# First stage of a fused gated cross-attention kernel: a ring of 15 chunks, tanh over runs of five chunks, weight rows spread over the batches

## The reference

```
txt_proj = jnp.einsum('btd,de->bte', textual_features, Ws)
feat_proj = jnp.einsum('bfd,de->bfe', features, W)
h = jnp.tanh(txt_proj[:, None, :, :] + feat_proj[:, :, None, :] + b[None, None, :, :][..., 0, :])
rho = jnp.einsum('bftd,d->bft', h, w[:, 0])
rho = rho + (1.0 - qm)[:, None, :] * NEG
att = jax.nn.softmax(rho, axis=-1)
txt_h = jnp.einsum('bft,btd->bfd', att, textual_features)
w_s = jnp.tanh(jnp.einsum('bfd,od->bfo', txt_h, Wcw) + bcw)
b_s = jnp.tanh(jnp.einsum('bfd,od->bfo', txt_h, Wcb) + bcb)
return w_s * features + b_s
```

## Time and profile before

| | us |
|---|---|
| median of 3 runs | 2029.7 |
| lowest, highest run | 2028.11, 2811.3 |
| the profiled execution | 2029.61 |
| its span in the trace | 2027.6 |
| main loop of stage A: first unit's tanh starts, last starts | 93.5, 951.3 |
| granted clock over the span | 0.965 of 2.4 GHz |

### The profile page before, as it was taken

How to read it: one execution, slowest core, us unless ns; L and a number is a source line. 1 busy time by engine, 2 the same in 40 slices (tenths; PEclk the granted TensorE clock), 3 DMA queues, 4 the chain that set the end, 5 groups by cost and what they waited for, 6 DMA issues and landing times.

```text
span 2027.6 us, 24744 instructions
## 1 busy us (share of the span) xinstructions
PE 1626.4 (80%) x9638; PEld 733.6 (36%) x9638; DVE 1744.2 (86%) x2631; ACT 1483.3 (73%) x1109; POOL 633.2 (31%) x476
## 2 busy tenths in 40 slices
PE   6868955697668857875789959999999968888886
PEld 4212211131112212221344436666666623433332
DVE  5899999999999988896778768888887779999994
ACT  4899999999999999998344735555554466665660
POOL 1000000000000000000351247666666537677773
PEclk9999999999999999999799979999999989999997
DMA  5001100020000010000676752333331111111111
GB/s 195 1 18 35 58 6 1 21 78 16 1 1 6 21 47 1 1 11 1 238 278 219 253 167 90 107 110 104 110 102 61 58 39 53 55 52 52 63 52 53
DMA packets 104294, 143.67 MB, mean 71 GB/s; under 512 B 7790, under 2 KB 61166, under 8 KB 103794
## 3 DMA queue, kind: packets, MB, share of 16 engines
q1 hardware_dynamic: 104178, 142.09, 20.9%
HBM read 91.74 MB, written 50.33 MB: 70 GB/s over the span
## 4 chain that ended last, share of the span: by engine, by line
ACT 42%; PE 33%; DVE 12%; POOL 7%; issue 4%; DMA 2%; POOLq 0%; SPq 0%; DVEq 0%; ACTq 0%
ACT unit L514 38%; PE psum L1624 6%; PE psum L1658 5%; POOL hidden L1806 5%; PE psum L1610 4%; PE psum L1009 3%; PE psum L1015 3%; DVE unit L423 2%; POOL h L1789 2%; PE psum L1634 2%; PE psum L1683 2%; DVE psum L1416 2%; DMA xblk<-xnT_scratch 2%; DVE hmax_parts L1425 2%; PE psum L1651 1%
## 5 line engine op out<-in xcount | busy, mean ns | idle before, releaser
L514 ACT ACTIVATE unit<-unit 128x4096 f32<-128x4096 f32 x244 | 857.5, 3615 | 0.5 <-DVE unit L423 0.3
L423 DVE TENSOR_SCALAR unit<-feat_proj,text_proj 128x1024 f32<-128x1024 f32 x976 | 668.0, 749 | 66.3 <-PE psum L639 64.5
L639 PE MATMUL psum<-unit,w_pad 128*32 128x512 f32 x3904 | 471.6, 601 | 236.3 <-ACT unit L514 236.3
L639 PEld LDWEIGHTS psum<-unit,w_pad 128*32 128x32 f32 x3904 | 102.3, 109 | 556.6 <-ACT unit L514 399.5
L680 POOL TENSOR_SCALAR red<-red 128x8 f32<-128x8 f32 x4 | 2.0, 508 | 531.5 <-DVE red L321 531.5
L1683 PE MATMUL psum<-xq_block,w_q 128*128 128x512 bf16 x512 | 132.7, 405 | 38.8 <-ACT hidden L1577 38.8
L1789 POOL TENSOR_TENSOR h<-h,arow 128x512 f32<-128x512 f32 x96 | 128.2, 1344 | 92.2 <-ACT h L1558 92.2
L1720 PE MATMUL psum<-w_q,hidden_q 128*128 128x512 fp8e4 x512 | 122.2, 394 | 29.7 <-DVE hidden_q L1449 29.7
L1806 POOL TENSOR_TENSOR hidden<-hidden,srow 128x2048 f32<-128x2048 f32 x32 | 130.4, 4074 | 27.1 <-ACT srow L1593 21.0
L680 POOL TENSOR_SCALAR rstd<-mv 128x8 f32<-128x8 f32 (+1 forms) x5 | 1.7, 334 | 412.4 <-DVE mv L216 412.4
L547 PE MATMUL psum<-xnT,W_sb 128*128 128x512 f32 x256 | 125.2, 617 | 2.1 <-ACT xnT L465 2.1
(11 more groups left out here) (243 smaller groups left out, 2780.0 us busy)
## 6 DMA issues: line engine op xcount, KB each, us to landing
h_scratch<-h SPq DMA_DIRECT2D x44, 512.0 KB, 3.1
hin<-h_scratch SPq DMA_DIRECT2D x32, 704.0 KB, 4.6
xin<-in_x SPq DMA_DIRECT2D x8, 1024.0 KB, 6.7
tern_in<-in_w1T SPq DMA_DIRECT2D x16, 512.0 KB, 5.5
tern_in<-in_w2T SPq DMA_DIRECT2D x16, 512.0 KB, 5.5
x<-in_x SPq DMA_DIRECT2D x16, 512.0 KB, 3.6
x_scratch<-x SPq DMA_DIRECT2D x32, 256.0 KB, 2.0
x3in<-x_scratch SPq DMA_DIRECT2D x31, 256.0 KB, 2.8
```

Of the source, the lines that this page charges most:

```text
L423: ins = ve.tensor_scalar(units[:, n % 3, k, :], FP[:, bi % 2, k, :], TP[:, k, n:n + 1], None, ALU.add)
L514: ac.activation(units[:, n % 3], units[:, n % 3], ACT.Tanh).then_inc(unit_tanh, 1)
L639: mm = te.matmul(psum[k * TG:(k + 1) * TG, 3 + 2 * grp + half, :], w_pad[:, k, TG - 1 - tt:2 * TG - 1 - tt], units[:, n % 3, k, half * BAN ...
```

## The change

Stage A's ring is cut into 15 chunks instead of three units, and the loops on ACT and PE go by **runs** of five chunks instead of units of four. What a chunk holds and what is added to it stays.

- DVE still adds four chunks per unit, but signals `unit_added` after each, and waits by chunk: chunk q needs the run that held chunk q - 15 to be through PE.
- ACT: 976 chunks in 195 runs of five, and one of one; one ACTIVATE over 5120 columns per run, when its five chunks are added.
- PE: per run, both halves, in each the five chunks in order; `unit_mm` counts runs. A run's chunks are at column groups k, k+1, k+2, k+3, k. What stood behind a unit's calls (`besides`) now stands behind the run that holds the unit's last chunk.
- ROW_SLOTS: four blocks in batch 0 (t = 14, 19, 24, 29), three in batches 1 and 2 (46, 51, 56), twelve in batch 3 (0, 5, ... 55), spacing five.

```diff
-    units = sb("unit", [P, 3, KC, SEQ], stack=pa)
+    units = sb("unit", [P, CHUNKS, SEQ], stack=pa)
...
-    ROW_SLOTS = [TXT * bi + p for bi in range(NB) for p in (37, 41, 45, 49, 53, 57)][:NROW]
+    ROW_SLOTS = ([TXT * bi + p for bi, ps in enumerate(((14, 19, 24, 29), (46, 51, 56), (46, 51, 56))) for p in ps]
+                 + [TXT * (NB - 1) + p for p in range(0, 60, 5)])
...
+    NCHUNK = (NU - RAMP) * KC
+
+    def runs_with(q):
+        return q // RUN + 1
+
+    def runs_of_unit(n):
+        return runs_with((n - RAMP) * KC + KC - 1)
...
         def rho_copy(bi, grp, half):
-            V.wait_ge(unit_mm, bi * TXT + (grp + 1) * TG - RAMP)
+            V.wait_ge(unit_mm, runs_of_unit(bi * TXT + (grp + 1) * TG - 1))
...
             V.wait_ge(fp_copied, (bi + 1) * 2 * KC)
-            V.wait_ge(unit_mm, n - 2 - RAMP)
-            if n < RAMP + 3:
-                V.wait_ge(ramp_mm, 2 * (RAMP - SLOTS // 2 + n - RAMP + 1))
             for k in range(KC):
-                ins = ve.tensor_scalar(units[:, n % 3, k, :], FP[:, bi % 2, k, :], TP[:, k, n:n + 1], None, ALU.add)
-            ins.then_inc(unit_added, 1)
+                q = (n - RAMP) * KC + k
+                if q >= CHUNKS:
+                    V.wait_ge(unit_mm, runs_with(q - CHUNKS))
+                elif q < SLOTS // 2 * KC:
+                    V.wait_ge(ramp_mm, 2 * (RAMP - SLOTS // 2 + q // KC + 1))
+                ve.tensor_scalar(units[:, q % CHUNKS, :], FP[:, bi % 2, k, :], TP[:, k, n:n + 1], None,
+                                 ALU.add).then_inc(unit_added, 1)
...
-            A.wait_ge(unit_added, n + 1 - RAMP)
-            ac.activation(units[:, n % 3], units[:, n % 3], ACT.Tanh).then_inc(unit_tanh, 1)
+            for q0 in range((n - RAMP) * KC, (n - RAMP + 1) * KC):
+                if q0 % RUN == 0:
+                    q1 = min(q0 + RUN, NCHUNK)
+                    row = units[:, q0 % CHUNKS:q0 % CHUNKS + q1 - q0, :]
+                    A.wait_ge(unit_added, q1)
+                    ac.activation(row, row, ACT.Tanh).then_inc(unit_tanh, 1)
...
+        for q0 in range(0, NCHUNK, RUN):
+            q1 = min(q0 + RUN, NCHUNK)
+            T.wait_ge(unit_tanh, runs_with(q0))
+            for half in range(2):
+                for q in range(q0, q1):
+                    mm = unit_rho(q, half)
+            mm.then_inc(unit_mm, 1)
+            for q in range(q0, q1):
+                if q % KC == KC - 1:
+                    besides(RAMP + q // KC)
```

## The result

The changed kernel takes 2074.47 us (median of 4 runs, 2072.32 to 2077.54) against 2029.7 for the kernel before: a ratio of 1.0221, 95% interval 1.0204 to 1.0237. It is 45 us slower. One run of the kernel before, 2811.3 us, counts as slow and is left out of its median and of the ratio. The profiled execution took 2072.32 us, with a span of 2070.3, 42.7 more than before.

The account below looks back on a forecast made before the run. ACT's tanhs bound the kernel, with PE nearly full in four dense stretches. From 2029.6 us, minus 4.5 for fewer tanhs, plus 42 of ACT waiting, plus 2 at the end, gave 2069, taken as 2068, range 2052 to 2086.

Parts of the forecast that it names:

- the busiest column group: Main case: on PE, the column group with most calls sets a run's time; 2052 to 2086 us, chance 0.83.
- A run on PE: Stage A on PE: ten calls, 8 passes in the fullest group instead of 4, 1.72 us more, so 3.65 to its end.
- Where ACT idles: Stage A's dense stretches: PE over by 1.5 and 11.2 us per batch 0 to 2, 9.6 in batch 3; 42 us lost.
- The credit for two runs in a row: On PE, a run directly following another may start two passes early in groups already free, credited 0.86 us.
- the ring's 1.4 us to spare: Stage A's chunk loop through PE, DVE and ACT takes 11.7 us of three run times, 13.1, lending at most 1.4.
- rival 2: PE's granted clock falls more often, each fall costing PE 1.7 us; ten outside spare time give 2085; chance 0.05.
- ACT's gain: Stage A on ACT: 196 tanhs instead of 244, each saving 0.094 us, 4.5 us gained.
- the end: After the last tanh, PE finishes 3.6 to 4.4 us later instead of 1.93; 2 us lost.
- Rival 1: Column groups share a run's passes, so a run steps at 2.29 us, PE never binds; 2025 us, chance 0.11.
- the 2070.3 that I gave as 2%: Threshold a measurement can tell, about 2% on the slow side; chances slower 0.37, same 0.61, faster 0.02.

## Why the prediction was right

The forecast was 2068 us, within 2052 to 2086, by the busiest column group; the time is 2074.47. Point by point:

**A run on PE.** Predicted 3.65 us to its end and a 3.58 step; measured 3.62 and 3.55. Two experiments change that count alone, in both directions, and the time follows: 4 calls down to 3 in the changed kernel gives back 40 us, 2 up to 4 in the kernel before costs 150.

**Where ACT idles.** Predicted 42 us, 11.3 in each of batches 0 to 2 and 8.2 in batch 3, and none in t = 0 to 25. The idle times in ACT's timeline add up to 10.3, 12.5, 11.2 and 9.5, 43.4 together; from t = 27 on they are 9.0, 11.2, 11.2 and 9.1, 40.4 together. The largest stand where they were expected, here in batches 0 and 3:

```profile
199.56 21.92 ACT L531 ACTIVATE unit<-unit 128x5120 f32<-128x5120 f32 x5 [2.94 <-DVE unit L436]
222.71 17.56 ACT L531 ACTIVATE unit<-unit 128x5120 f32<-128x5120 f32 x4 [1.23 <-DVE unit L436]
...
921.24 75.28 ACT L531 ACTIVATE unit<-unit 128x5120 f32<-128x5120 f32 x18 [3.57 <-DVE unit L436]
```

**The credit for two runs in a row** was too small: I let the next run start two passes early, 0.86 us, and two runs take 5.37 us at 190.81, where 2 x 3.55 would be 7.1. That is 12 slots instead of 16, four passes early, since the groups that are done take all their calls of the next run. It does not always come: at 215.01 two runs take 5.77, and where the second run's tanh is late it is less. The swapped halves showed why: the credit was counted with one waiting pass to a group, and there are more. In t = 38 to 54 of batch 0 the runs that follow each other start 5.3 us early in all, where I credited 2.6, and ACT idles 9.0 in that batch where I had 11.3. In batches 1 and 2 they start 3.6 and 4.3 us early, and ACT still idles the forecast 11.2, so 1 to 2 us went there that my sum left out. DVE's other work eating the ring's 1.4 us to spare is a candidate that no run tested. That the total came out at 43.4 against 42 is in part luck: the larger credit, this loss and the 3.0 us of stalls below cancelled.

**What I missed.** Each time ACT stalls, the 0.10 us by which a tanh overlaps the next is lost too: 34 stalls, 3.4 us. The page shows it, 856.9 busy us for the 196 tanhs, where 195 steps of 4.37 and the last tanh's 0.94 make 853. And four stalls stand in t = 0 to 25, where I expected none: 1.01 and 0.35 us at 106.7 and 111.5, 1.25 at 360.4 in batch 1, and 0.37 at 841.3 in batch 3. The first three stand behind stretches of the lower clock of rival 2. The first such stretch, after the ramp (PE alone, changed kernel):

```profile
core 0: us, PE busy (x), PEclk, DMA share, GB/s
92.00:96.00 4.00, 1.07 (x8) 0.91 0.00 0
96.00:100.00 4.00, 2.97 (x16) 0.50 0.01 4
100.00:104.00 4.00, 4.00 (x16) 0.73 0.00 0
```

The granted clock is 0.50, 1.2 of 2.4 GHz, from 96 on, and the first run takes 6.14 us, longer than ACT's 4.37. Ahead of the second fall PE had idled 2.10 us, while ACT took the exp of batch 0: the clock is 0.50 from 352 to 354, and DVE waits 4.01 us for the run that started at 350.51. So rival 2 came true twice, for some 2.6 us of ACT's waits; that the clock is the whole of these stalls was not tested. The clock falls in stage A of the kernel before too, around 93, 98 and 790, and there ACT does not wait. In the changed kernel's dense windows, with one group working alone half of each run, the clock is 1.00, and over the span it is 0.968 against 0.965 before.

**ACT's gain and the end.** Predicted 4.5 us gained. The loop from the first tanh's start to the last one's end takes 904.0 us against 861.4 before: 43.4 idle, less 0.3 before, plus 3.4 for lost overlaps, minus 4.5, is 42.0 of these 42.6. So the 4.5 us are there, hidden in a loss ten times as large, and the kernel that hands chunks back one by one gets most of them out. The end cost 0.8 us by the idle time ahead of the last exp (7.75 against 6.97), not the 2 I gave it, as the one-chunk run lies wholly beside the run ahead of it:

```profile
995.62 3.65 PE L654 MATMUL psum<-unit,w_pad 128*32 128x512 f32 x24 [0.74 <-ACT unit L531]
```

**The rivals.** Rival 1 (the groups share passes out) would have a run at 2.3 us and idle time on PE in the dense stretches; a run takes 3.62 and PE is busy 59.66 of 59.80 there. The Trainium skill ("TensorE: Matmul & The Clock Gate", Part 3, "What overlaps and what doesn't") has matmuls start and end in strict program order. The runs here disagree: by that order a run would need twelve slots of 0.43, 5.2 us (the prediction's 4.9 was too low), and it takes 3.62; in the slots above three groups finish ahead of calls that stand before theirs, and swapping the halves changes nothing.

**The size.** The sum made 2069 and the profiled execution took 2072.3, 3.2 more. The lost overlaps are 3.4 of it and ACT's idle time, 43.4 against 42, another 1.3; the end (0.8 instead of 2) and a main loop that starts 1.0 earlier (92.5 against 93.5) go the other way, and under 1 us stays unassigned. So the mechanism was right and the size a little low. The profiled execution and the median both lie above the 2070.3 that I gave as 2%, on the side that I gave 0.37 against 0.61.

## What to carry to other kernels

Where matmuls are packed side by side into column groups, count calls per group, not calls: a piece takes its largest group's. Here the step from eight calls to ten was 25% more calls and took PE from 1.86 to 3.55 us, 91% more. If the groups' results are summed anyway, the group need not follow the data's index. And before merging instructions on the engine that binds, to save 0.09 us each, look at the stretches where another engine is nearly full (here PE, at 94% and 92%): there a piece that grows on that engine is paid in full.

## What the runs showed of the hardware

- Column groups of TensorE work through their calls on their own. Ten calls split 4, 2, 2, 2 and eight split 4, 2, 2, 0 both take 3.62 us, ten split 3, 3, 2, 2 take 2.77, eight split 2, 2, 2, 2 took 1.93: 0.43 us a pass of 512 columns (f32) in the largest group, plus about 0.2.
- A call for a busy group does not hold up later calls for other groups, as far as these runs queue them: with a chunk's two calls (four passes) adjacent in one group, a run still takes 3.62 us. Two runs in a row fill the groups across their boundary, 40 records in 5.37 us.
- A stall of ACT costs 0.10 us more than its idle time, the overlap of back-to-back ACTIVATEs (4.47 us each, 4.37 a step).
